# Four layers of attention and feed-forward on one Trainium2 core: maxima units first in a step, second weights begun inside the norm and the gate

## What is computed

```python
x = x + L0_xattn(ctx, layernorm(x))      # queries x, keys [x; ctx]: 8 heads of 64, 1101 keys
x = x + L0_ffn(layernorm(x))             # 8 experts, F = 512, each token to one expert
x = x + L1_xattn(layernorm(x), ctx)      # 77 keys, 16 heads of 16
x = x + L1_ffn(layernorm(x))             # self attention 16 x 16, then 8 experts, F = 1024, top 2
x = x + L2_xattn(layernorm(x), ctx)
x = x + L2_ffn(layernorm(x))             # 8 experts, F = 1024, top 2
x = x + L3_xattn(layernorm(x), ctx)
x = x + L3_ffn(layernorm(x))             # FP4-rounded gated feed-forward
return x
```

## Time and profile before

| what | us |
|---|---|
| runs, median (lowest to highest) of 3 | 2851.25 (2847.18 to 2856.83) |
| the profiled execution, its own time | 2855.69 |
| its span, first to last instruction | 2854.0 |
| TensorE busy | 2215.2 (78% of the span) |
| VectorE busy | 1264.8 (44%) |
| ScalarE busy | 1095.0 (38%) |
| GpSimd busy | 682.6 (24%) |
| mean granted TensorE clock | 0.874 |

### The profile page before, as it was taken

How to read it: one execution, slowest core, us unless ns; L and a number is a source line. 1 busy time by engine, 2 the same in 40 slices (tenths; PEclk the granted TensorE clock), 3 DMA queues, 4 the chain that set the end, 5 groups by cost and what they waited for, 6 DMA issues and landing times. The chain is left out here.

```text
span 2854.0 us, 36597 instructions
## 1 busy us (share of the span) xinstructions
PE 2215.2 (78%) x12230; PEld 1308.4 (46%) x12231; DVE 1264.8 (44%) x2406; ACT 1095.0 (38%) x2197; POOL 682.6 (24%) x581
## 2 busy tenths in 40 slices
PE   4899999943948658999994599967739998481687
PEld 2333333333923422333333499953329998231354
DVE  4654444065154566778723300024540000549565
ACT  2424444421315303666672244424414443151211
POOL 0238888801410130000000122210002222104011
PEclk9999999975968875999997699988959999685699
DMA  1000000023510260242403466630156664100001
GB/s 60 4 1 12 14 10 15 20 63 104 178 50 1 68 119 5 35 56 31 60 1 124 158 196 199 201 129 18 55 169 198 201 195 139 53 1 31 10 15 35
DMA packets 145976, 216.36 MB, mean 76 GB/s; under 512 B 39856, under 2 KB 101996, under 8 KB 145852
## 3 DMA queue, kind: packets, MB, share of 16 engines
q1 hardware_dynamic: 136156, 188.27, 24.3%
q0 software_dynamic: 9696, 26.49, 2.5%
HBM read 182.00 MB, written 30.15 MB: 74 GB/s over the span
## 5 line engine op out<-in xcount | busy, mean ns | idle before, releaser
L2841 PE MATMUL experts_up_ps<-experts_rowT,experts_w 128*128 128x128 f32 x2864 | 341.1, 277 | 0.0
L1802 DVE TENSOR_REDUCE heads_part_max<-heads_shared_ps 128x2 f32<-128x1024 f32 x256 | 299.9, 1219 | 90.3 <-PE heads_shared_ps L1719 90.3
L1786 ACT ACTIVATE heads_probs<-heads_score_ps 128x512 f32<-128x512 f32 x512 | 266.4, 603 | 191.2 <-PE heads_score_ps L1741 191.2
L2841 PEld LDWEIGHTS experts_up_ps<-experts_rowT,experts_w 128*128 128x128 f32 x2864 | 333.0, 194 | 0.2
L2991 DVE TENSOR_TENSOR experts_y<-experts_down_ps,experts_b_now 128x256 f32<-128x256 f32 x78 | 33.1, 424 | 556.3 <-PE experts_down_ps L2851 556.3
L1320 POOL TENSOR_TENSOR core_xT<-core_xT,heads_probs 128x1024 f32<-128x1024 f32 (+1 forms) x112 | 264.4, 2361 | 32.4 <-ACT heads_probs L1489 22.7
L2901 ACT ACTIVATE experts_hT<-experts_up_ps,experts_b_now 128x128 f32<-128x128 f32 x624 | 222.9, 367 | 47.8 <-PE experts_up_ps L2841 10.5
L1528 DVE TENSOR_REDUCE heads_part_max<-heads_shared_ps 128x1 f32<-128x512 f32 x256 | 164.5, 685 | 153.5 <-PE heads_shared_ps L1362 153.4
L1741 PE MATMUL heads_score_ps<-heads_q,heads_k 66*128 66x512 f32 x512 | 197.8, 474 | 29.8 <-ACT heads_probs L1786 25.6
L2790 POOL DMA_INDIRECT y_dram<-experts_y,experts_index x101 | 99.4, 984 | 456.2 <-DVE experts_y L2991 411.5
L1489 ACT ACTIVATE heads_probs<-heads_score_ps 128x1024 f32<-128x1024 f32 x128 | 131.0, 1023 | 186.9 <-PE heads_score_ps L1389 177.1
(11 more groups left out here) (561 smaller groups left out, 3241.7 us busy)
## 6 DMA issues: line engine op xcount, KB each, us to landing
experts_w<-in_L_ffn_W SPq DMA_DIRECT2D x39, 1024.0 KB, 5.2
experts_w<-in_L_ffn_w SPq DMA_DIRECT2D x39, 1024.0 KB, 5.2
experts_w<-in_L_ffn_W SPq DMA_DIRECT2D x23, 512.0 KB, 4.0
core_xT<-y_dram SPq DMA_DIRECT2D x20, 512.0 KB, 4.8
experts_b_now<-in_L_ffn_b SPq DMA_DIRECT2D x78, 128.0 KB, 2.9
heads_q<-l_queries SPq DMA_DIRECT2D x32, 256.0 KB, 11.8
heads_k<-l_keys SPq DMA_DIRECT2D x32, 256.0 KB, 14.2
l1f_w<-in_L_ffn_W SPq DMA_DIRECT2D x8, 1024.0 KB, 11.8
```

The costliest lines, as they stand in the source:

```text
L1786: act.activation(probs[:, t % SLOTS_OF_PROBS, r, :], score_ps[:, i % RING, :], ACT.Exp, scale=SC).then_inc(exp_done, 1)
L1802: dve.tensor_reduce(part_max[:, g % 2, 2 * pair:2 * pair + 2, s, x], two, AX.X, ALU.max).then_inc(shared_read, 1)
L2841: done = pe.matmul(up_ps[:, f % 4, 0:SLOT], w1_sb[:, u, c, f * P:(f + 1) * P], rowT[:, u % 2, c, :], start=(c == 0), stop=(c == DC - 1))
```

## The change

1. In `pair_attention` the maxima units of a step come ahead of its scores on TensorE, and ahead of WEIGH in the table; WEIGH and TURN stay behind the scores.
2. The stages that began the second weights are gone. SyncE issues these loads inside the layer norm, after the gain and shift where there are any: all eight in L0, five in L1 and L2, and the last three at the start of the gate's stage.
3. The gate's weights and bias are loaded by ScalarE's queue instead of SyncE's, and so are the first bias and the columns of gain and shift in `sparse_experts`.

The diff, cut:

```diff
@@ layer_norm
-        if gain is not None:
-            @block.sync
-            def _(sp):
+        @block.sync
+        def _(sp):
+            if gain is not None:
                 sp.dma_start(affine[:, 0, :], column(gain, DC)).then_inc(loaded, 16)
                 sp.dma_start(affine[:, 1, :], column(shift, DC)).then_inc(loaded, 16)
+            if second_weights is not None:
+                second_weights.begin(sp)
@@ gate
         @block.sync
         def _(sp):
-            if transposed:
-                sp.dma_start(w_raw[:], w).then_inc(loaded, 16)
-            else:
-                sp.wait_ge(w_cleared, 1)
-                sp.dma_start(w_sb[:, :, 0:E], chunked(w)).then_inc(loaded, 16)
-            if bias is not None:
-                sp.dma_start(bias_sb[:], across(bias, E)).then_inc(loaded, 16)
+            if second_weights is not None:
+                second_weights.go_on(sp)
             sp.wait_ge(loaded, 32 if bias is not None else 16)
...
         @block.scalar
         def _(act):
+            if transposed:
+                act.dma_start(w_raw[:], w).then_inc(loaded, 16)
+            else:
+                act.wait_ge(w_cleared, 1)
+                act.dma_start(w_sb[:, :, 0:E], chunked(w)).then_inc(loaded, 16)
+            if bias is not None:
+                act.dma_start(bias_sb[:], across(bias, E)).then_inc(loaded, 16)
             act.wait_ge(all_done, 1)
@@ pair_attention
-        if s in WEIGH_AT and 0 <= HALVES * g + WEIGH_AT[s] - (s == 3) * HALVES < HALVES * PAIRS:
-            work_at[t].append((WEIGH, HALVES * g + WEIGH_AT[s] - (s == 3) * HALVES))
         if t < STEPS:
             work_at[t] += left[0:2]
             left = left[2:]
+        if s in WEIGH_AT and 0 <= HALVES * g + WEIGH_AT[s] - (s == 3) * HALVES < HALVES * PAIRS:
+            work_at[t].append((WEIGH, HALVES * g + WEIGH_AT[s] - (s == 3) * HALVES))
         if s == TURN_AT and g + 1 < PAIRS:
             work_at[t].append((TURN, g + 1))
...
             for t in range(STEPS):
+                for item in work_at[t]:
+                    if item[0] == PEAK:
+                        share(item)
                 score(t)
                 for item in work_at[t]:
-                    share(item)
+                    if item[0] != PEAK:
+                        share(item)
                 if t:
                     value(t - 1)
@@ SecondWeights
-    def begin(self, nc, name, w2):
-        with Stage(nc, name) as st:
...
-                for e in range(E):
-                    sp.dma_start(self.sb[:, e, :, :], w2[e].rearrange("(c p) d -> p c d", p=P)).then_inc(self.loaded, 16)
+    def load(self, sp, experts):
+        for e in experts:
+            sp.dma_start(self.sb[:, e, :, :], self.w2[e].rearrange("(c p) d -> p c d", p=P)).then_inc(self.loaded, 16)
+
+    def begin(self, sp):
+        self.load(sp, range(0, self.in_norm))
+
+    def go_on(self, sp):
+        self.load(sp, range(self.in_norm, E))
@@ sparse_experts
-            if affine is not None:
-                for x in range(2):
-                    sp.dma_start(columns[:, x, :], column(affine[x], DC)).then_inc(const_loaded, 16)
             if has_bias:
-
-                sp.dma_start(b1_raw[:], b1).then_inc(b1_out, 16)
                 sp.wait_ge(b1_copied, 1)
...
         @block.scalar
         def _(act):
+            if has_bias:
+                act.dma_start(b1_raw[:], b1).then_inc(b1_out, 16)
+            if affine is not None:
+                for x in range(2):
+                    act.dma_start(columns[:, x, :], column(affine[x], DC)).then_inc(const_loaded, 16)
             if has_bias:
                 act.wait_ge(b1_turned, 1)
@@ build (layer 1; layer 0 has SecondWeights(..., E), layer 2 has 5 as here)
-                second = SecondWeights(keep, 4 * D)
-                second.begin(nc, "w2of1", a["L1_ffn_W2"])
+                second = SecondWeights(keep, 4 * D, a["L1_ffn_W2"], 5)
```

More of the change, by code:

```diff
@@ L816, in __init__, with gate @@
         self.top = stage.sb("top", [P, choices, NT])
-def gate(nc, core, name, routing, w, transposed, bias, kind, probs_out=None):
+def gate(nc, core, name, routing, w, transposed, bias, kind, probs_out=None, second_weights=None):
     SIDE = P // 4
@@ L2605, with __init__ @@
 class SecondWeights:
-    def __init__(self, stage, F):
+    def __init__(self, stage, F, w2, in_norm):
         self.sb = stage.sb("w2", [P, E, F // P, D])
         self.loaded = stage.sem("w2_loaded")
-    def begin(self, nc, name, w2):
-        with Stage(nc, name) as st:
-            block = st.block()
-            @block.sync
-            def _(sp):
-                for e in range(E):
-                    sp.dma_start(self.sb[:, e, :, :], w2[e].rearrange("(c p) d -> p c d", p=P)).then_inc(self.loaded, 16)
+        self.w2, self.in_norm = w2, in_norm
+    def load(self, sp, experts):
[5 more added lines that the diff above has]
+        self.load(sp, range(self.in_norm, E))
 def sparse_experts(nc, core, name, routing, rows, F, w1, second, b1, b2, func, affine=None):
@@ L3037, in build @@
                 rows = moe.sb("rows", [P, NT, D])
-                second = SecondWeights(moe, 2 * D)
-                second.begin(nc, "w2of0", a["L0_ffn_W2"])
-                layer_norm(nc, core, "ln0f", rows_out=rows)
+                second = SecondWeights(moe, 2 * D, a["L0_ffn_W2"], E)
+                layer_norm(nc, core, "ln0f", rows_out=rows, second_weights=second)
                 routing = Routing(moe, 1)
@@ L3072, in build @@
                 hats = keep.sb("hats", [P, NT, D])
[L3073 to L3075 removed]
+                second = SecondWeights(keep, 4 * D, a["L1_ffn_W2"], 5)
+                layer_norm(nc, core, "ln1g", rows_out=hats, gain=a["L1_ffn_ln2_g"], shift=a["L1_ffn_ln2_b"], source=rows,
+                           second_weights=second)
                 add_rows(nc, core, "add1", rows)
@@ L3078, in build @@
                     routing = Routing(moe, 2)
-                    gate(nc, core, "gate1", routing, a["L1_ffn_gate_w"], False, a["L1_ffn_gate_b"], "pair_softmax")
+                    gate(nc, core, "gate1", routing, a["L1_ffn_gate_w"], False, a["L1_ffn_gate_b"], "pair_softmax",
+                         second_weights=second)
                     sparse_experts(nc, core, "experts1", routing, hats, 4 * D,
@@ L3090, in build @@
                 rows = moe.sb("rows", [P, NT, D])
-                second = SecondWeights(moe, 4 * D)
-                second.begin(nc, "w2of2", a["L2_ffn_w2"])
-                layer_norm(nc, core, "ln2f", rows_out=rows)
+                second = SecondWeights(moe, 4 * D, a["L2_ffn_w2"], 5)
+                layer_norm(nc, core, "ln2f", rows_out=rows, second_weights=second)
                 routing = Routing(moe, 2)
-                gate(nc, core, "gate2", routing, a["L2_ffn_gate_w"], True, a["L2_ffn_gate_b"], "pair_probs")
+                gate(nc, core, "gate2", routing, a["L2_ffn_gate_w"], True, a["L2_ffn_gate_b"], "pair_probs",
+                     second_weights=second)
                 sparse_experts(nc, core, "experts2", routing, rows, 4 * D,
```

3 lines of the change are left out of this document (1 added, 2 removed).

## The result

| | before | changed |
|---|---|---|
| median of the runs, us | 2854.03 (4 runs, 2847.18 to 2856.83) | 2806.41 (4 runs, 2795.09 to 2814.48) |
| ratio, with its 95% interval | | 0.9831 (0.9806 to 0.9855) |
| the profiled execution, us | 2855.69, span 2854.0 | 2795.09, span 2793.3 |

A forecast was written before the change was run, and what follows sets the result against it. TensorE's own order of work bounds the first self attention; three load-only stages wait on a full DMA queue. Terms -44.2 - 0.3 + 4.3 - 8.5 = -48.7 take 2855.69 to 2807.0, against the median 2802.5 us, range 2788 to 2821.

The forecast's parts named there:

- The three stages, -44.2: Ahead of the three norms: removing the load-only stages saves 7.46 + 18.47 + 18.32 us, as the norms hide the issues.
- Affine loads, -0.3: Second norm's gain and shift loads, issued ahead of the large ones, land early: 0 to 2.5 us gained, 0.3 taken.
- I take 2 us for each: Gate's small loads beside the 3 MB stream: 2 us for each of the last two layers, +4.3 together, ends 0 and +10.8.
- the sign of the rival: In the gates: a gate load landing after 8 us would make "The gate starves" right, chance 0.14.
- The maxima, -8.5: First self attention: maxima units first save 5.4 us in 108 plain steps and 3.1 in 13 with weights' sums; ends -16, +11.
- P to M: Attention step, start of the scores' bf16 row-maxima pair to start of the maxima units: 0.29 us in the new order.
- M to K: Attention step, start of the maxima units to start of the scores' keys pair: falls from 0.33 to 0.21 us.
- The step with W: Attention step that also holds the weights' sums: 3.32 us in place of 3.56, in 13 steps.
- K to V: Attention step, start of the scores' keys pair to start of the values' pair: 0.95 us in the new order.
- V to P: Attention step, start of the values' pair to start of the next scores' row-maxima pair: 1.01 us in the new order.
- The order of the maxima costs: Rival in the first self attention: both weight loads exposed, +11 in place of -8.5, 2822 us; chance 0.13.
- The gate starves: Rival in the gates: small loads land as late as the affine loads did, +10.8 for +4.3, 2809 us; chance 0.14.

The follow-up runs named there:

- the third profile: Changed kernel run a third time without edits, on the chip of the run with the gate's loads in the norm: 2806.26 us, ratio 0.9832.
- the repeats: The changed kernel run twice more without edits, for further profiles: 2803.09 us (ratio 0.9811) and 2806.26 us (0.9832).
- the second profile of the change: Changed kernel run once more without edits, for another profile: 2803.09 us, ratio 0.9811.

## Why the prediction was right, point by point

**The three stages, -44.2: right.** VectorE is idle for 0.55 and 0.57 us ahead of the norms of layers 2 and 1 and for 1.47 ahead of layer 0's, and the cover held: the norm of layer 1 lasts 16.54 us with five loads issued in it. With eight it doesn't (19.88), so how many it holds matters. I had bounded the five issues by 11.3 us; they took 9.3 (1500.06 to 1509.32).

**Affine loads, -0.3: right** (16.80 to 16.54 us).

**"No row shows small loads from ScalarE beside a stream ... I take 2 us for each": the term mis-sized.** It measured +4.4 and +3.4 us from issue to use in the profile of the change, and 8.3 over the two stretches with the affine gain in them, against 4.3. My upper end of 10.8 from the affine loads was the better neighbour than GpSimd's gathers, which I took as nearest. The bias landed 7.5 to 7.8 us behind its issue in the three profiles, just under the 8 that I had named as the sign of the rival. The runs with SyncE waiting or issuing the small ones first put it down to the order of the issues: all of it in layer 1 (375.0 and 375.3 us, 375.1 before); in layer 2 1.2 us are left, and the change's own profiles differ by 2.5 there, so the times from issue to use (3.5 us, 5.5 to 6.3 in the change) say more than the stretch.

**The maxima, -8.5: the sign and the sum of parts right, the size too small by 3.7** (heads0 450.7 and 450.4 from 462.9 at the same clock; the 448.3 of the third profile is the clock's, see the repeats). "P to M ... 0.29" was 0.04, and "M to K falls ... to 0.21" was 0.42: 0.46 us together for 0.50, so a plain step of 2.42 for 2.46. The step with W was right (3.29 for 3.32), and so were K to V (0.95) and V to P (1.01). What the step sum leaves out is that the gain is not all kept. In the stretch of norm and gate behind the attention, from the norm's first instruction to the gate's copy on ScalarE, it takes 19.7 to 20.0 us in all eight profiles with the new order and the gate's loads issued in the gate, and 17.6 to 18.3 in four with an older order or with the maxima in the middle, at a clock of 0.60 and 0.67 for the first 20 us of the change and of before. Why the clock of the norm follows the order of the stage ahead of it is open.

**The rivals.** "The order of the maxima costs" is excluded by the steps. "The gate starves" came nearer in price than the forecast (8.3 of 10.8 us), but the condition that I gave it, ScalarE's loads ending only with the large ones issued ahead, is not what the landings show. The clock stayed at 1.00 in the attention. The two terms' errors, 4 us too little cost at the gates and 4 us too little gain at the maxima, nearly cancelled: that the gain came within 1.1 us of the forecast is luck in part, and no proof of its parts. The time itself is 3.9 us above the 2802.5, as the median of before rose by 2.8 with its fourth run. That the sum held against the medians, and not against the profiles (60.6 us apart), rests on the second self attention.

## To carry to other kernels

A small load that somebody waits for should be issued ahead of the large ones, best a whole stage ahead, whatever queue either is on: in layer 1 the same loads cost 2.9 us ahead of three large ones, 7.5 beside them, and no wait at all when begun in the norm. A stage that only issues transfers can go into a neighbour as long as the neighbour outlasts the issues, so count how many it covers. And compare two profiles stretch by stretch, the untouched stretches first: here one of them differed by 14 us for no reason of the change.

## What the hardware showed unexpectedly

- Behind V, a bf16 pair of matmuls and then an f32 pair on the same rows start 0.04 us apart and take 0.46 us together; in the other order 0.34 us apart and 0.57 us.
- One 8 KB load's issue took SyncE 3.98 us behind three 1 MB ones, against 0.37 alone.
- Small loads on ScalarE's queue, issued just behind the last of eight 1 MB loads on SyncE's, were in use 5.6 us later, against 2.6 us before, while 0.40 MB of the large ones had still to move: late, but not last.
- With no gap in TensorE's work, the granted clock stayed at 0.50 for over 40 us in one execution; in another it had come back within the same stretch. In the cross attention of layer 2 its mean was 0.60 over 30 us in the second profile of the change. Between that profile and the first, 23.5 us apart, these two stages differ by 15.7 and 10.5 us.
